# Layer-1 self-attention of a Perceiver kernel: output product by groups, a second bank of column sums, value products between query/key products, idle products at the head

## What is computed

```python
x = x + _L1_attn_ref(_layernorm(x, axis=-1), L1_attn_w_qkv, L1_attn_w_o)

def _L1_attn_ref(x, w_qkv, w_o):
    qkv = jnp.einsum('bsh,hf->bsf', x, w_qkv)
    qkv = qkv.reshape(b, s, 3, N_HEADS, D_HEAD)
    ...
    scores = jnp.einsum('bhqd,bhkd->bhqk', q, k) / jnp.sqrt(jnp.float32(D_HEAD))
    probs = jax.nn.softmax(scores, axis=-1)
    values = jnp.einsum('bhqk,bhkd->bhkd', probs, v)
    values = values.transpose(0, 2, 1, 3).reshape(b, s, N_HEADS * D_HEAD)
    out = jnp.einsum('bsf,fh->bsh', values, w_o)
    return out
```

## Time and profile before

| | |
|---|---|
| median of three runs | 1258.19 us |
| time of the profiled execution | 1260.3 us |
| its span in the profile | 1258.2 us |
| mean granted clock of TensorE in the span | 0.947 of full speed |
| busy, PE / DVE / ACT / POOL | 1088.8 / 693.3 / 480.2 / 204.7 us |
| the stretch that L1A takes, from x of the part before to its own | 293.0 to 386.4 us |

### The profile page before, as it was taken

The page is one execution under the profiler, slowest core; times in us unless marked ns, Lnnn a source line. Parts: engine busy times, 40 slices in busy tenths (PEclk is TensorE's granted clock), DMA queues, the critical chain, the costliest instruction groups (busy, mean ns, idle before and its releaser), DMA issues.

```text
span 1258.2 us, 22810 instructions
## 1 busy us (share of the span) xinstructions
PE 1088.8 (87%) x9325; PEld 755.7 (60%) x9325; DVE 693.3 (55%) x1534; ACT 480.2 (38%) x1054; POOL 204.7 (16%) x188
## 2 busy tenths in 40 slices
PE   6988899986885999999999997885889684777998
PEld 5866666655654556555555665763545453675886
DVE  3544357773335767665566625555574857454332
ACT  1111147771220345555555683532334231121232
POOL 0003100000002000000000000017868885000000
PEclk9998999998987999999999999997999887878999
DMA  9012300004003000000000002025443432004551
GB/s 382 7 73 78 118 2 2 2 2 163 1 1 125 35 1 2 2 2 2 2 2 2 2 3 82 1 77 141 125 151 95 128 106 76 15 1 188 218 213 60
DMA packets 16182, 84.38 MB, mean 67 GB/s; under 512 B 3152, under 2 KB 3664, under 8 KB 12368
## 3 DMA queue, kind: packets, MB, share of 16 engines
q1 hardware_dynamic: 7888, 57.75, 12.0%
q0 software_dynamic: 8192, 25.17, 7.1%
HBM read 82.65 MB, written 0.26 MB: 66 GB/s over the span
## 4 chain that ended last, share of the span: by engine, by line
PE 66%; POOL 14%; DVE 11%; issue 5%; ACT 3%; DMA 1%; POOLq 0%; SPq 0%; DVEq 0%; ACTq 0%
POOL L2F_rows L2516 9%; PE L2X_bank_ring L1771 7%; PE L2X_bank_ring L1787 6%; PE L2X_bank_read L1801 5%; PE L2X_bank_ring L1710 4%; PE L1X_banks_scores L916 3%; PE L2X_bank_ring L1719 2%; PE L0X_bank_k L457 2%; PE L3F_bank_y L3382 2%; PE L0X_bank_moments L468 2%; PE L3F_bank_gathered L3331 2%; PE L3F_bank_gate_up L3342 2%; POOL L2F_z_exp L2492 2%; PE L1X_bank_proj L893 2%; PE L1A_bank_qk L1181 2%
## 5 line engine op out<-in xcount | busy, mean ns | idle before, releaser
L2068 DVE TENSOR_REDUCE L2X_max_parts<-L2X_bank_ring 128x1 f32<-128x512 f32 x256 | 158.3, 684 | 85.7 <-PE L2X_bank_ring L1771 85.6
L1979 ACT ACTIVATE L2X_context_exp<-L2X_bank_ring 128x384 f32<-128x384 f32 (+1 forms) x384 | 144.2, 463 | 62.3 <-PE L2X_bank_ring L1787 59.6
L2516 POOL DMA_INDIRECT L2F_rows<-in_L2F_embed_dram,L2F_expert x128 | 133.3, 1041 | 61.0 <-issue 36.7
L1771 PE MATMUL L2X_bank_ring<-L2X_context_kT,L2X_q_masked 32*128 32x512 f32 x512 | 96.9, 630 | 0.0
L1024 ACT ACTIVATE L1X_probs<-L1X_clipped,L1X_drop,L1X_keep 128x1024 f32<-128x1024 f32 x64 | 77.8, 1239 | 30.6 <-DVE L1X_clipped L1084 23.5
L1084 DVE TENSOR_SCALAR L1X_clipped<-L1X_banks_scores 128x1024 f32<-128x1024 f32 x64 | 75.4, 1220 | 24.6 <-PE L1X_banks_scores L916 22.9
L1787 PE MATMUL L2X_bank_ring<-L2X_q_and_max,L2X_context_kT 32*128 32x384 f32 (+1 forms) x768 | 85.9, 497 | 0.0
L1801 PE MATMUL L2X_bank_read<-L2X_context_exp,L2X_context_v_ones 128*32 128x128 f32 x2048 | 75.8, 277 | 1.1 <-ACT L2X_context_exp L1979 0.8
L1801 PEld LDWEIGHTS L2X_bank_read<-L2X_context_exp,L2X_context_v_ones 128*32 128x32 f32 x2048 | 50.2, 109 | 43.8 <-issue 33.4
L2745 DVE SCALAR_TENSOR_TENSOR x<-L2F_rows,L2F_expert_weight,x 128x256 f32<-128x256 f32 x128 | 62.4, 488 | 4.6
L2621 ACT ACTIVATE L3X_k_features<-L2F_banks_pair 128x1024 f32<-128x1024 f32 x32 | 32.8, 1024 | 79.9 <-remote 57.8
(11 more groups left out here) (625 smaller groups left out, 2044.8 us busy)
## 6 DMA issues: line engine op xcount, KB each, us to landing
L3F_expert_weights<-in_L3F_experts_dram SPq DMA_DIRECT2D x16, 1280.0 KB, 5.6
L1A_groups<-in_L1A_groups_dram SPq DMA_DIRECT2D x3, 1536.0 KB, 9.5
ctxT<-in_ctxT_dram SPq DMA_DIRECT2D x8, 512.0 KB, 11.8
L0X_tokens<-in_L0X_tokens_dram SPq DMA_DIRECT2D x8, 512.0 KB, 15.0
slot<-in_L1A_dram SPq DMA_DIRECT2D x1, 3584.0 KB, 11.3
slot<-in_L0F_dram SPq DMA_DIRECT2D x1, 3072.0 KB, 10.7
slot<-in_L2A_dram SPq DMA_DIRECT2D x1, 3072.0 KB, 10.8
slot<-in_L2F_dram SPq DMA_DIRECT2D x1, 2476.5 KB, 8.8
```

Of the source, the lines that this page charges most:

```text
L1771: nc.tensor.matmul(bank[:, :], qm[32 * g:32 * g + 32, b, c, j, :], cT[32 * g:32 * g + 32, s % 3, blk * 512:(blk + 1) * 512], start=True, s ...
L1979: nc.scalar.activation(ex[:, n % NE, g, 0:width(s)], bank_of(s_e, done(n) + g + 1)[:, 0:width(s)], ACT.Exp, scale=SCALE).then_inc(s_e, 1)
L2068: nc.vector.tensor_reduce(parts[:, j, g, blk:blk + 1], bank_of(s_ft, n)[:, :], AX, ALU.max).then_inc(s_ft, 1)
L2516: pool.indirect_dma_start(out=rows[:, r, k, :], out_offset=None, in_=env.dram["L2F_embed"], in_offset=bass.IndirectOffsetOnAxis(idx[:, b, ...
```

## The change

The products with `w_o` are cut into parts by unit (`out_part`): the two parts of group g-1 stand behind the scores of group g, ahead of the next group's projections, and the last two at the end. Only the first product of the bank carries the start flag. `bank_c` becomes a pair, the second of which is the head's bank `bank_x`, so units take turns, and a column sum waits for the scaling of the unit before the last. The two value jobs of a group stand behind the second and the fourth head's query/key products. The head gets 14 products of the identity with itself ahead of its transposes.

```diff
--- before.py
+++ after.py
@@ -1136,7 +1136,7 @@
     SCALE = P ** -0.5
     bank_x, bank_o = L.bank("xT"), L.bank("out")
     bank_qk = [L.bank(f"qk{j}") for j in range(2)]
-    bank_v, bank_c = L.bank("v"), L.bank("colsum")
+    bank_v, bank_c = L.bank("v"), (L.bank("colsum"), bank_x)
     bank_s = [L.bank(f"scores{j}") for j in range(2)]
     head = Head(L, bank_x)
     more = L.sb("groups", [P, NG - 1, 3 * HG * KC * P])
@@ -1181,15 +1181,18 @@
                         i = nc.tensor.matmul(bank_qk[n % 2][:, part * T:(part + 1) * T], wt(g, part, h, k), head.xT[:, k, :],
                                              start=(k == 0), stop=(k == KC - 1))
                 i.then_inc(s_qk, 1)
-            for j in range(HG // 2):
-                n = g * (HG // 2) + j
-                if n >= 1:
-                    pe.wait_ge(s_vc, n)
-                for h in range(2):
-                    for k in range(KC):
-                        i = nc.tensor.matmul(bank_v[:, h * T:(h + 1) * T], wt(g, 2, 2 * j + h, k), head.xT[:, k, :],
-                                             start=(k == 0), stop=(k == KC - 1))
-                i.then_inc(s_v, 1)
+                if h % 2:
+                    project_values(g, h // 2)
+
+        def project_values(g, j):
+            n = g * (HG // 2) + j
+            if n >= 1:
+                pe.wait_ge(s_vc, n)
+            for h in range(2):
+                for k in range(KC):
+                    i = nc.tensor.matmul(bank_v[:, h * T:(h + 1) * T], wt(g, 2, 2 * j + h, k), head.xT[:, k, :],
+                                         start=(k == 0), stop=(k == KC - 1))
+            i.then_inc(s_v, 1)
 
         def scores(u):
             g, b = units[u]
@@ -1203,29 +1206,36 @@
 
         def column_sums(u):
             pe.wait_ge(s_pn, u + 1)
-            if u:
-                pe.wait_ge(s_val, u)
-
-            nc.tensor.matmul(bank_c[:, :], env.const("ones"), pn[:, u % 2, :, :].rearrange("p h t -> p (h t)"),
+            if u >= 2:
+                pe.wait_ge(s_val, u - 1)
+            nc.tensor.matmul(bank_c[u % 2][:, :], env.const("ones"), pn[:, u % 2, :, :].rearrange("p h t -> p (h t)"),
                              start=True, stop=True).then_inc(s_c, 1)
 
+        def out_part(u):
+            g, b = units[u]
+            pe.wait_ge(s_val, u + 1)
+            for h in range(g * HG, (g + 1) * HG):
+                i = nc.tensor.matmul(bank_o[:, b * D:(b + 1) * D], val[:, h, b * P:(b + 1) * P], w("w_o")[:, h * D:(h + 1) * D],
+                                     start=(h == 0 and b == 0), stop=(h == 15), skip_group_check=True)
+            if u == len(units) - 1:
+                i.then_inc(s_out, 1)
+
         env.wait_weights(pe, "L1A")
-        head.tensor(pe)
+        head.tensor(pe, 14)
         pe.wait_ge(head.s_xT, 1)
         project_group(0)
         for g in range(NG):
             for b in range(B):
                 scores(g * B + b)
+            if g:
+                for b in range(B):
+                    out_part((g - 1) * B + b)
             if g + 1 < NG:
                 project_group(g + 1)
             for b in range(B):
                 column_sums(g * B + b)
-        pe.wait_ge(s_val, len(units))
         for b in range(B):
-            for h in range(16):
-                i = nc.tensor.matmul(bank_o[:, b * D:(b + 1) * D], val[:, h, b * P:(b + 1) * P], w("w_o")[:, h * D:(h + 1) * D],
-                                     start=(h == 0), stop=(h == 15))
-        i.then_inc(s_out, 1)
+            out_part((NG - 1) * B + b)
 
     @block.gpsimd
     def _(pool):
@@ -1292,7 +1302,7 @@
             g, b = units[u]
             dve.wait_ge(s_c, u + 1)
             nc.vector.tensor_tensor(val[:, g * HG:(g + 1) * HG, b * P:(b + 1) * P], vT[:, g % 2, :, b * P:(b + 1) * P],
-                                    bank_c[:, :].rearrange("p (h t) -> p h t", h=HG), ALU.mult).then_inc(s_val, 1)
+                                    bank_c[u % 2][:, :].rearrange("p (h t) -> p h t", h=HG), ALU.mult).then_inc(s_val, 1)
 
         copy_values(0)
         for g in range(NG):
```

## The result

The changed kernel takes 1244.11 us (median of four, 1239.03 to 1244.93) against 1257.91 of the kernel before beside it: ratio 0.9879, interval 0.9858 to 0.9900, so 1.0 to 1.4% faster. The forecast was 1243.2. The profiled execution took 1244.93 us, 15.4 less than that of before.

What follows compares the result with a forecast made beforehand. L1A (layer-1 self-attention) was taken as bound by PE throughout, by its products and own gaps. Terms 3.76 + 1.0 + 3.1 + 7.7 - 0.3 - 0.3 = 15.0 us off 1258.19 gave 1243.2 us, range 1240 to 1248.

Steps and rivals of the forecast that it cites:

- x to the first scores: Start of layer-1 self-attention: head 0.3 us worse, first group's value jobs 0.94 us better.
- head: Start of layer-1 self-attention: 14 idle products delay projections 2.6 us and save 2.0 of slow clock, 0.3 us worse.
- first value jobs: First group: second value job no longer waits for DVE's copy, 0.94 us off.
- first scores to second: From the first group's scores to the next group's: 14.1 us instead of 16.36.
- second to third, third to last: Later groups, scores to next scores: 17.6 us each with output products included, against 16.36 before.
- hand-over: Output products at three new places in front of something else: 0.1 us added each, 0.3 us in all.
- last scores to x: End of layer-1 self-attention: 10.7 us plus 6.9 moved forward, 17.6 against 25.34, so 7.7 us off.
- C: Rival, in the groups: waits move to DVE's scaling instead of vanishing, 7.9 us lost again, 1251 us; chance 0.08.
- the slow part of the projections: Head: first projections take 8.92 us for 6.91, so idle products can save 2.01 us.
- the lag of the clock: Head: the clock rises 5.9 us after PE resumes, at 299.0; with 3.8 us the head would be 0.4 better.
- D: Rival: the clock falls inside the groups, slower than before, 1261 us with 36 us at half clock; chance 0.02.
- B: Rival: slow-clock terms at end and head partly an accident of the profiled execution, 3 to 4 us less gained, 1247; chance 0.14.

Runs made afterwards that it cites:

- e5: The kernel before with only the value jobs moved between the query/key jobs: 1255.41 us, ratio 0.9963.
- e6: The kernel before with only the second bank of column sums: 1255.92 us, ratio 0.9965.
- e7: The kernel before with only the output products by group: 1252.10 us, ratio 0.9934.
- e1: The change run again with no edit: 1243.79 us, ratio 0.9877 to the kernel before.
- e3: The change with 7 idle products at the head instead of 14: 1243.85 us, ratio 0.9885 to the kernel before.
- e4: The change with 28 idle products at the head instead of 14: 1246.24 us in one run.
- e8: The kernel before with only the 14 idle products at the head: 1260.80 us, ratio 1.0003.
- e11: The change with 7 idle products instead of 14, a second trace: its execution took 1243.06 us.
- e2: The change without the 14 idle products at the head: 1243.24 us, ratio 0.9875 to the kernel before.
- e9: The kernel before, unchanged, a second trace: 1260.1 us.
- e10: The kernel before with only the second bank of column sums, a second trace: stretch of layer-1 self-attention 87.26 us.

## Why the prediction was right

The terms, from the traces before and after:

| term | forecast | measured |
|---|---|---|
| x to the first scores (head, first value jobs) | -0.64 | 18.30 to 17.56: -0.74 |
| first scores to second | -2.30 | 16.36 to 13.86: -2.50 |
| second to third, third to last, less 3.45 of output, with a hand-over each | -2.2 each | 16.36 to 13.87: -2.49 each |
| last scores to x, with the 6.9 moved and one hand-over | -7.6 | 25.34 to 10.80 + 6.9: -7.6 |
| sum | -15.0 | -15.9 |

**Waits.** Each wait went where it was forecast to go, and none came back in another place (C): e5, e6 and e7 show that each part takes away its own. The experiments' own gains, against the mean stretch of 93.8 us of before, are 3.7, 6.5, 7.2 and for the idle products nothing. Their sum, 17.4, is near the 16.2 and 17.3 us of the whole change, but the nearness is partly chance: the slow clock of the end, about 2 us, is in both the second and the third and can be had only once, while the first, and the idle products, each had an end more than 1 us longer than before's. By medians of the whole the parts gain 5.4, 4.9, 8.7 and 0.0 us, about 19 against the change's 14.9.

**The price that was off in the groups** is the hand-over. I had charged 0.3 us for three new places, and left the 0.11 us from values to sums and the 0.07 behind the sums standing. They were no hand-overs: eight value records take 1.84 us behind a wait (the longest of them 0.483 us, the median 0.379) and 1.72 without (339.61 to 341.33, all 0.379). With the waits their after-effects went, 0.2 us in each of three groups, and in two of the three places the charge was not called on; at the end it was (10.80 against 10.7). That is 0.8 us of the 0.9 between 15.0 and 15.9, and the head is the rest.

**The head** was forecast 0.3 us dearer and stands at 0.2 between the two first traces (2.22 later, 2.01 back). That agreement is luck. The forecast took the slow part of the projections, 2.01 us, from one trace; the six others without idle products lost 2.5 to 2.6 there. And it took the lag of the clock near the two long ones, 5.9 us; the first trace after had 5.2, but the five others with idle products (e1, e3, e4, e8, e11) had 3.0, under the 3.8 that was put aside. Among traces whose clock ahead of L1A fell alike, 14 idle products earn 1.3 us (e2 against e1; e8 against e6, e7, e9 and e10), and 7 earn 2.9 (e2 against e3 and e11), since they end when the normalised x is ready. So "most likely earn nothing" was wrong for the usual case, by 1.6 us in this term.

**The whole.** The forecast of 1243.2 is 0.9 us from the measured 1244.11, and this nearness is partly luck as well. The medians gain 13.8 us, and 14.9 in e1; the stretch gained 15.9 between the first traces and 17.6 between e9 and e1 (94.16 to 76.52), whose clocks ahead of L1A fell alike. Parts of the kernel whose lists did not change gave part of the difference back (last section); the rest is not explained.

**The clock in the groups (D)** stayed at 1.00. The section of the Trainium skill that spoke for a swing ("A second HAM failure mode: psum-queue depth-cycling", in "TensorE: Matmul & The Clock Gate") is about cycling through banks with small idle pieces between. The change cycles through eight banks but has no idle pieces left, 71.1 us at 1.00, so its traces do not test that; the trace of before, with two gaps near 0.8 us in each group and 64.7 us at 1.00, is the one that does not bear it out. The only fall of the clock within that trace's stretch stood at its end, behind the gap of 2.57 us.

**B**, that the gain is partly an accident of the profiled execution, falls: the end is slow in both traces of the kernel before, and later runs, on other chips, put it at 1258.67 (11 runs), 1260.77 (26) and 1258.52 us (one), above the 1258.19 that I started from.

## What to carry to other kernels

Read a recurring wait from start to start of the rows around it, not from its bracket; the longer first record behind it (0.1 us here) goes with it. Products that depend on finished work only (here the output products of the last group) are best put where the engine would wait for something young; here that closed the gap of 2.57 us, and with it the slow clock of the end went in seven traces of seven. Size idle products by the time the engine has, at the pitch of the half clock, since in all six traces they began at it: 14 records fitted in 3.1 us, 28 did not. Compare a term that hangs on the clock between traces whose clock just before was the same, and look at the pieces of a stretch, not only at its length: in e8 a gain at one end hid behind a loss at the other.

## What was not expected of the hardware

The whole time does not follow the stretch within 2 us. With seven idle products the stretch is 1.6 to 2.6 us shorter than with 14, the median of the whole the same. The profiled executions alone, of which the stretches are, do differ: 1243.85 and 1243.06 us with 7, 1245.30 and 1244.93 with 14. But that of e2, without idle products and with the longest stretch of the five, took 1242.75. Part of the difference is found behind L1A: the cross-attention of layer 2, whose list is the same in all kernels, takes 360.5 to 360.8 us in six traces (before, e9, e2, e6, e10, e8) and 361.8 to 362.2 in seven (after, e1, e3, e11, e4, e5, e7). In slices of 20 us, each of these seven has one slice behind the first with a granted clock of 0.91 or 0.92, either 40 to 60 us or 340 to 360 us into that part, and none of the six has one; the first slice lies between 0.84 and 0.92 in all. The slice from 40 us on, of the change again (e1) and then of the change without idle products (e2), the clock again in the column before the last two:

```profile
428.70:448.70 20.00, 20.00 (x132) 11.04 (x133) 12.21 (x23) 7.76 (x19) 0.00 (x0) 0.91 0.00 1
```

```profile
427.60:447.60 20.00, 20.00 (x142) 11.44 (x141) 12.80 (x25) 8.94 (x23) 0.00 (x0) 1.00 0.00 1
```

What decides whether the clock falls there was not tried. It is open, and so is whether the change makes it likelier: its two traces are of the second kind, but so are those of two single parts without idle products (e5, e7). It costs about 1.4 us of the 16. Two more unchanged parts come in two lengths: the cross-attention of layer 1, ahead of L1A, takes 152.3 us in the first traces of before and after and 154.6 to 154.7 in the other eleven, and the self-attention of layer 2 takes 61.0 us in nine and 61.9 to 62.3 in four (after, e3, e11, e8). So a difference of one or two microseconds in the whole, from a single trace, does not speak for the part that was changed.
